# One pair sum of each attention unit moved from GpSimd to VectorE, and the clearing of the output bank moved behind two score matmuls

## The reference, cut to what matters

```
q = (xn @ Wq.T).reshape(B, Tx, 16, 32)      # k, v from the context likewise
scores = einsum('bqhs,bkhs->bhqk', q, k) / sqrt(32)
attn = softmax(scores, axis=-1)
out = einsum('bhqk,bkhs->bqhs', attn, v)
x = x + out @ Wo.T + bo
x = x + mx_quantize(layernorm(x)) @ mx_quantize(w).T + bias
```

## Time and profile before

| | |
|---|---|
| median of 3 executions | 4435.17 us (4431.02 to 4442.58) |
| the profiled execution: time, span | 4433.29 us, 4431.5 us |
| TensorE busy | 4264.6 us, 96% of the span, granted clock 0.998 |
| VectorE busy | 3400.1 us, 77% |
| ScalarE busy | 2850.1 us, 64% |
| GpSimd busy | 2938.9 us, 66% |

### The profile page before, as it was taken

How to read it: one execution, slowest core, us unless ns; L and a number is a source line. 1 busy time by engine, 2 the same in 40 slices (tenths; PEclk the granted TensorE clock), 3 DMA queues, 4 the chain that set the end, 5 groups by cost and what they waited for, 6 DMA issues and landing times.

```text
span 4431.5 us, 89201 instructions
## 1 busy us (share of the span) xinstructions
PE 4264.6 (96%) x36496; PEld 1486.4 (34%) x36496; DVE 3400.1 (77%) x3967; ACT 2850.1 (64%) x5184; POOL 2938.9 (66%) x1830
## 2 busy tenths in 40 slices
PE   4999999999999999999999999999999999999998
PEld 2322343223432234322342223422234222342223
DVE  5788667886688865888658886688866888668875
ACT  3387744877448864478655886558755587546884
POOL 2299652996539954499534995359953599426993
PEclk9999999999999999999999999999999999999999
DMA  5256642657326573356733566335664366543654
GB/s 182 71 121 125 158 143 62 125 119 187 115 62 128 115 200 102 71 117 124 191 101 77 115 125 184 106 79 119 124 174 110 78 122 127 167 112 78 126 124 107
DMA packets 193708, 539.67 MB, mean 122 GB/s; under 512 B 28737, under 2 KB 102785, under 8 KB 152082
## 3 DMA queue, kind: packets, MB, share of 16 engines
q0 software_dynamic: 43776, 318.79, 36.0%
q1 hardware_dynamic: 149522, 215.17, 15.6%
HBM read 118.32 MB, written 21.01 MB: 31 GB/s over the span
## 4 chain that ended last, share of the span: by engine, by line
PE 66%; DVE 20%; ACT 4%; DMA 3%; POOL 3%; issue 3%; SPq 0%; DVEq 0%; ACTq 0%; POOLq 0%
PE banks L1114 17%; PE banks L1126 16%; PE banks L1022 16%; PE banks L1082 11%; DVE max_parts L663 11%; PE banks L1157 4%; PE banks L991 2%; ACT region L892 2%; DMA sums<-wkT_wvT_wqT 1%; PE banks L1016 1%; POOL wkT_wvT_wqT L453 1%; DVE amax L611 1%; ACT values L972 1%; DVE x_stats L573 1%; DVE region L801 1%
## 5 line engine op out<-in xcount | busy, mean ns | idle before, releaser
L663 DVE TENSOR_REDUCE max_parts<-banks 128x2 f32<-128x1024 f32 x2048 | 2397.1, 1217 | 409.4 <-PE banks L1082 393.4
L892 ACT ACTIVATE region<-banks 128x512 f32<-128x512 f32 x4096 | 2190.5, 607 | 452.5 <-PE banks L1114 401.6
L453 POOL TENSOR_TENSOR wkT_wvT_wqT<-region 128x1024 f32<-128x1024 f32 x528 | 1313.0, 2632 | 464.6 <-PE banks L1126 273.0
L1114 PE MATMUL banks<-queries_stacked,keys_stacked 98*32 98x512 f16 x16384 | 1264.2, 382 | 12.5 <-ACT values L876 6.2
L1126 PE MATMUL banks<-region,values 128*32 128x512 f32 x8192 | 1076.0, 599 | 17.7 <-ACT region L892 14.2
L1082 PE MATMUL banks<-keys_stacked,queries_stacked 33*128 33x512 f16 x4096 | 724.0, 385 | 31.8 <-DVE max_parts L663 28.3
L1114 PEld LDWEIGHTS banks<-queries_stacked,keys_stacked 98*32 98x32 f16 x16384 | 401.3, 95 | 1000.3 <-ACT region L892 599.4
L1022 PE MATMUL banks<-region,wkT_wvT_wqT 128*128 128x512 f16 x2304 | 556.7, 380 | 13.2 <-DMA wkT_wvT_wqT<-weights_split 10.6
L1082 PEld LDWEIGHTS banks<-keys_stacked,queries_stacked 33*128 33x128 f16 x4096 | 184.2, 93 | 649.1 <-issue 354.1
L453 POOL TENSOR_TENSOR sums<-region 128x1024 f32<-128x1024 f32 x144 | 373.0, 2729 | 9.1 <-ACT region L892 9.1
L433 POOL TENSOR_TENSOR region<-row_sums_inverse,region 128x512 f16<-128x512 f32 x80 | 93.0, 1163 | 429.5 <-ACT region L855 428.9
(11 more groups left out here) (99 smaller groups left out, 3232.4 us busy)
## 6 DMA issues: line engine op xcount, KB each, us to landing
wdT<-wkT_wvT_wqT POOLq DMA_DIRECT2D x96, 1024.0 KB, 12.0
wkT_wvT_wqT<-wkT_wvT_wqT POOLq DMA_DIRECT2D x80, 1024.0 KB, 7.3
sums<-wkT_wvT_wqT POOLq DMA_DIRECT2D x72, 1024.0 KB, 7.4
wkT_wvT_wqT<-sums POOLq DMA_DIRECT2D x40, 1024.0 KB, 7.4
region<-in_x SPq DMA_DIRECT2D x24, 1024.0 KB, 8.6
wkT_wvT_wqT<-weights_split SPq DMA_DIRECT2D x8, 3072.0 KB, 20.6
keys_stacked<-region SPq DMA_DIRECT2D x384, 64.0 KB, 2.0
keys_stacked<-sums SPq DMA_DIRECT2D x384, 64.0 KB, 2.0
```

Source lines behind the costliest of these rows:

```text
L453: e.tensor_tensor(SUMS[dst][:, half], PR[i][:, half], PR[i + 1][:, half], ALU.add).then_inc(s_pr, 1)
L663: e.tensor_reduce(mpart[:, buf, :, a, t, c], MXB[parity], AX.X, ALU.max).then_inc(s_mxd, 1)
L892: e.activation(PR[u % 4][:, j * HALF:j * HALF + HALF], score_bank(m % NU, kt, j)[0], ACT.Exp, scale=SCALE).then_inc(s_ex, 1)
L1114: mm = e.matmul(dst[HD * t:HD * t + HD, :], KA[0:STR, ds(ka + (j * C + (u + 1) * P + HD * t), HD)], QA[0:STR, ds(qa[j], HALF)], start=True ...
```

## The change

1. For every unit but the last of a batch, pair 2 (tiles 4 and 5) leaves GpSimd's list. VectorE makes its two halves (`third_pair`), the first after the reductions of the max parts of step 4 and the second after those of step 5. It waits for pairs 0 and 1 (`s_pr`), for TensorE to have read the buffer that it overwrites (`s_pv`), and for the exponentials of tile 5 (`s_ex`). GpSimd, instead of making pair 2, waits until both halves are done, ahead of pair 3.
2. The clearing of OB moves from the front of step 0 to behind step 0's first two scores (behind all four in the last unit, where `ahead` holds), ahead of the weighing.

```diff
@@ gpsimd, units but the last
-                        e.wait_ge(s_pv, n * KT + 4 + (3 if g + q == 0 else 4))
-                        pair(2, two)
                         if g + q > 0:
                             e.wait_ge(s_ac2, late * 16)
+
+                        e.wait_ge(s_pr, n * 14 + 2 + 6)
                         pair(3, three)
                         merge(1, 2, two)
@@ vector, unit(g, q, last)
+                    def third_pair(h):
+                        two = buffers(n)[2]
+                        half = ds(2 * HALF * h, 2 * HALF)
+                        if h == 0:
+                            e.wait_ge(s_pr, m * 14 + 2 + 4)
+                            e.wait_ge(s_pv, m * KT + 4 + (3 if n == 0 else 4))
+                        e.wait_ge(s_ex, m * (KT * J) + 5 * J + 2 * h + 4)
+                        e.tensor_tensor(SUMS[two][:, half], PR[0][:, half], PR[1][:, half], ALU.add).then_inc(s_pr, 1)
+
                     end = last and q == 1
                     if not end:
                         for t in range(QT):
                             max_row(idx + 8 + 2 * t, 1 - q, QT + t)
+                            if t < 2:
+                                third_pair(t)
                         maxima(1 - q, n + 1, idx + 16)
@@ tensor, step(..., first=None)
                     if ahead:
                         score(2)
                         score(3)
+                    if first:
+                        clear(OB, *first)
                     if weigh:
                         mm = outputs()
@@ tensor, unit(g, q, last)
                             step(m, n, ex, ka, qa, v, u, t + 1, rows[u], sums=sums, fresh=fresh, closing=t == closing,
+                                 first=(s_oc, m + 1) if t == 0 else None,
                                  between=(lambda: turn_next(ex)) if t == 9 and not end else None)
-                    clear(OB, s_oc, m + 1)
```

More of the change, by code:

```diff
@@ L1091, in step @@
                 def step(m, n, ex, ka, qa, v, u, tile, row=None, after=None, sums=(), end=False, between=None, scores=True,
-                         weigh=True, fresh=None, closing=False):
+                         weigh=True, fresh=None, closing=False, first=None):
                     if row:
```

## The result

The changed kernel takes 4453.26 us (median of 9, 4448.85 to 4456.37), the kernel before 4437.27 us in the same comparison (median of 9): ratio **1.0038, 95% interval 1.0029 to 1.0048**, so 16 us slower. The forecast was 4460, range 4441 to 4486. Its profiled execution took 4449.46 us with a span of 4447.7, 16.2 us above the profiled execution of before.

The account below looks back on a forecast made before the run. The prediction took TensorE's chain as the bound, with VectorE as full in unit 0. Its terms, 6 + 13.6 + 6 = 25.6 us on 4433.3, gave 4458.9, or 4460.8 with 1.9 for the median; it said 4460, range 4441 to 4486.

Parts of the forecast that it names:

- The relief is worth nothing: GpSimd loses 264 us of pair sums, but waits for VectorE and starts pair 3 1.0 us later.
- Unit 0: VectorE has no gaps there, so its two added halves cost 1.7 us a unit, 13.6 us in all.
- 2.36 less 0.64 absorbed: In unit 0, of two halves' 2.36 us on VectorE, 0.64 is absorbed as for the row sums' inversion, leaving 1.7.
- Units 1 to 5: VectorE's gaps nearly take the two halves; 0.15 us a unit is lost, 6 us over 40 units.
- the second half makes step 6's start 0.27 us late: In units 1 to 5 step 6's reductions on VectorE start at 855.93 in place of 855.66.
- The border of units 6 and 7: GpSimd's pair 6 ends 0.75 us later, delaying unit 7's exponentials and first weighing: 6 us over 8 times.
- Edit 2: Moving the clearing gains 0: at unit 7's start TensorE still waits for the exponentials behind GpSimd's pair 6.
- if that cover were gone it would be 6.9 us: Without unit 7's wait for exponentials, moving the clearing would gain the 6.9 us wait for the outputs' copy.
- Rival (a): VectorE's sums and GpSimd's L497 exclude each other, up to 0.83 us in each of 40 units: 4494 us; chance 0.15.
- The room forecast, 1 us: GpSimd's L497 was to end about 1 us before VectorE's first half starts, so the two would not collide.
- Rival (b): No measurable change: unit 0 loses only 0.87 us, 7 us in all, the rest is absorbed: 4442 us; chance 0.19.
- Rival (c): Faster: idle time before clearings was TensorE's own loss, 22 us for OB, filled by scores: 4413 us; chance 0.06.

Follow-up runs that it names:

- e3: The full change, but in unit 0 of each batch GpSimd makes pair 2: 4441.34 us, ratio 1.0007 to the kernel before.
- e4: The full change in units 1 to 5 only; in units 0 and 6 GpSimd makes pair 2: 4440.36 us, ratio 1.0005 to the kernel before.
- e9: The kernel before, with VectorE making pairs 5 and 6 of unit 6 and pair 2 of units 1 to 6; clearing not moved: 4422.64 us, ratio 0.9965.
- The half dose: The full change, but in unit 0 VectorE makes only the first half of pair 2, GpSimd the second: 4445.08 us, ratio 1.0022 to the kernel before.
- e2: The kernel before with only the clearing moved, all pairs still on GpSimd: 4436.38 us, ratio 1.0000.
- e10: The kernel before, with VectorE making pairs 5 and 6 of unit 6, and the clearing moved: 4423.04 us, ratio 0.9966.
- e1: The full change with the clearing back at its old place: 4452.87 us, ratio 1.0037 to the kernel before.
- e6: e4 with GpSimd's normalisation L497 done twice, begun after step 4's first reduction (computes another result): 4456.07 us, ratio 1.0044 to the kernel before.

## Why the prediction was right, and which terms were not

The direction, the mechanism and the two places that pay were right; the sum of 25.6 us was 10 us too high. 6 of these are the term of units 1 to 5.

- **The relief is worth nothing.** Right: e3, e4 and e9 show no gain from it. GpSimd's 262 us less of work became idle time ahead of pair 3.
- **Unit 0, 1.7 us a batch, 13.6 us.** It measured 1.80 us, 14.4 us. The size was right, the reason half wrong: "2.36 less 0.64 absorbed" took the absorption of the inversion as a fixed amount. The half dose shows that about four fifths of each 1.14 us is paid. The inversion's own share, 0.87 of 1.51 or 0.58, did not hold here either; why the two differ is not shown. The two halves are 2.27 us of VectorE, not 2.36. (The last units have 40 pairs of such halves, not 80.)
- **Units 1 to 5, 0.15 us a unit, 6 us.** This term was mis-sized: it is 0. The step that failed is "the second half makes step 6's start 0.27 us late". It used 2.36 us for two reductions and 1.18 for a sum. But the recorded durations overlap by some 0.09 us where two operations follow each other. From reduction to sum it is 857.56 − 855.29 = 2.27 and from sum to reduction 1.14: 3.41 us, where 3.42 were free.
- **The border of units 6 and 7, 0.75 us a batch, 6 us.** It measured 0.67 us, 5.4 us, in the rows of batch 1. e4 shows that unit 6's pair is the cause. The prediction had it in the wait of 0.70 us, which was to grow to 1.4; that wait stayed, and the one before it, 0.22 us, which the prediction did not name, grew to 0.90.
- **Edit 2, 0.** Right in e2. But "if that cover were gone it would be 6.9 us" was wrong: the 6.9 us were idle time of the weight load while the array was busy, and e10, where the cover is gone, shows 0.
- **Rival (a), blocking.** It did not happen: the sums took 1.22 us in all 112 cases. The rows say why: in unit 2 L497 ended by 857.23, and the first half began at 857.56. The room forecast, 1 us, was 0.3 us there, and over the 40 units it goes from 0.9 us down to nothing by the recorded ends. In e1 one sum of the 112 began 0.22 us before L497 had ended, and took 1.31 us. So it was a near thing. The mechanism is real, as e6 shows. **Rival (b)** had unit 0 at 0.87 us and lost by that. **Rival (c)** is refuted by e2.

By the rows of batch 1 the terms come to 19.8 us, and the medians differ by 16.0. In the profiled executions the falls of the clock account for 1.5 us of the remainder; the rest has no cause shown.

## What to carry to other kernels

Relief of an engine is worth what is waited for at its end: ask at which single place another engine waits for it, and move the work there, not where it is easiest to fit. A piece moved into a gap must fit by start-to-start times, since the recorded durations of neighbours overlap, and each kind of unit has to be read by itself: one in eight had no gap, and it paid for about three quarters. The idle time of a weight load is to be read beside the matmuls of the same stretch: here the array was busy, and 6.9 us of it were no loss.

## What the runs showed of the hardware

**TensorE's clock at the start of unit 0.** In some batches, and not in others of the same execution, the granted clock falls to half, 1.2 in place of 2.4 GHz, for a few us. The kernel before at the start of unit 0 in batches 0 and 1; the columns are the stretch, its length, the busy times of the five engines, the granted clock, the DMA share and GB/s:

```profile
203.00:212.00 9.00, 8.46 (x81) 2.24 (x85) 3.13 (x4) 6.30 (x12) 4.72 (x2) 0.81 0.01 2
748.00:757.00 9.00, 8.31 (x97) 2.45 (x97) 4.51 (x5) 7.40 (x15) 4.69 (x2) 1.00 0.01 2
```

The same stretch of work has a mean granted clock of 0.81 once and of 1.00 once, with 81 matmuls recorded in place of 97. Within the fall it is half:

```profile
205.40:208.60 3.20, 3.18 (x22) 0.68 (x20) 0.00 (x0) 1.72 (x5) 1.89 (x1) 0.50 0.02 5
```

A weighing in batch 5 took 1.94 us, in batch 1 1.06:

```profile
2929.56 1.94 PE L1126 MATMUL banks<-region,values 128*32 128x512 f32 x8
```

```profile
750.81 1.06 PE L1126 MATMUL banks<-region,values 128*32 128x512 f32 x8
```

Ahead of it TensorE has two short waits, of 0.78 us before its first scores of the unit and of 0.35 us after them. They are the same in batches 0 and 5, where the clock falls, and in batch 1, where it does not. Before the change it fell there in batches 0, 5 and 6, after it in batch 0 alone, for twice as long. From the L671 of the front to that of unit 0 it is 33.54 us without a fall and 34.97 to 35.01 with one, so a fall costs 1.4 to 1.5 us; the long one cost 3.1. That is one reason why differences of 2 or 3 us between two kernels cannot be read from two profiles.

**GpSimd and VectorE.** One VectorE sum of two SBUF operands and one GpSimd multiplication exclude each other in both directions: 1.21 us became 1.47 and 1.27 became 2.14 (e6).
